# First cross-attention of a two-layer Perceiver step: query keys from 64-row products, a new order for keys and context chunks

## The reference

```python
scale = DH ** (-0.5)                       # DH = 64, HEADS = 16
q = split_heads(x @ Wq)                    # x is layer-normed before
k, v = split(context @ Wkv)                # both split into heads
k = concat(null_key, k); v = concat(null_value, v)
attn = softmax((q * scale) @ k.T)
out = (attn @ v).merge_heads() @ Wout      # then layer norm, residual
```

## Time and profile before

| | us |
|---|---|
| median of 3 runs | 510.11 (509.84 to 511.09) |
| the profiled execution | 510.38 |
| its span | 508.8 |
| TensorE busy (products) | 486.1 |
| VectorE busy | 256.5 |
| ScalarE busy | 233.8 |
| GpSimd busy | 74.4 |

### The profile page before, as it was taken

How to read it: one execution, slowest core, us unless ns; L and a number is a source line. 1 busy time by engine, 2 the same in 40 slices (tenths; PEclk the granted TensorE clock), 3 DMA queues, 4 the chain that set the end, 5 groups by cost and what they waited for, 6 DMA issues and landing times.

```text
span 508.8 us, 8527 instructions
## 1 busy us (share of the span) xinstructions
PE 486.1 (96%) x3600; PEld 415.5 (82%) x3600; DVE 256.5 (50%) x445; ACT 233.8 (46%) x410; POOL 74.4 (15%) x61
## 2 busy tenths in 40 slices
PE   6999999999999999999888999999999999889997
PEld 6987989899988989899775769976666789678697
DVE  2836231337055131310355987866555566358585
ACT  1737332346245233331134967606767353237772
POOL 2112000001010000000110434473000000004342
PEclk9979999999999999999999999999999999999999
DMA  8647000021420000000296999930000074254000
GB/s 320 227 170 250 21 1 1 1 84 50 200 82 1 1 0 1 1 1 2 77 423 265 399 408 408 379 124 1 2 1 1 1 318 180 84 225 189 0 1 10
DMA packets 12325, 62.50 MB, mean 123 GB/s; under 512 B 1183, under 2 KB 3615, under 8 KB 6400
## 3 DMA queue, kind: packets, MB, share of 16 engines
q1 hardware_dynamic: 9696, 52.17, 26.0%
q0 software_dynamic: 2592, 9.80, 5.5%
HBM read 61.84 MB, written 0.13 MB: 122 GB/s over the span
## 4 chain that ended last, share of the span: by engine, by line
PE 79%; DVE 7%; ACT 4%; POOL 4%; issue 3%; DMA 1%; POOLq 1%; SPq 0%; DVEq 0%; ACTq 0%
PE W L1316 18%; PE W L1277 15%; PE W L1460 8%; PE W L1546 6%; PE W L1507 5%; PE W L1214 3%; PE W L1258 3%; PE W L1293 3%; POOL w_lo L489 3%; PE W L1579 3%; PE W L1596 2%; PE W L1338 2%; POOL small L497 1%; ACT w_hi L545 1%; PE W L1351 1%
## 5 line engine op out<-in xcount | busy, mean ns | idle before, releaser
L1316 PE MATMUL W<-probs_turned_hi,ctx_split_hi 128*128 128x256 f32 x256 | 72.8, 285 | 0.1
L1316 PE MATMUL W<-probs_turned_hi,ctx_split_lo 128*128 128x256 f32 x256 | 72.4, 283 | 0.0
L1316 PE MATMUL W<-probs_turned_lo,ctx_split_hi 128*128 128x256 f32 x256 | 72.4, 283 | 0.0
L862 DVE TENSOR_TENSOR probs_turned_lo<-W,probs_turned_hi 128x512 fp32r<-128x512 f32 x32 | 20.6, 687 | 65.0 <-ACT probs_turned_hi L595 65.0
L1277 PE MATMUL W<-ctx_turned_hi,q_keys_hi 128*128 128x512 f32 x128 | 52.4, 409 | 0.0
L1507 PE MATMUL W<-w_hi,acts 128*128 128x256 f32 x272 | 50.8, 286 | 1.5 <-DVE acts L829 1.0
L1277 PE MATMUL W<-ctx_turned_hi,q_keys_lo 128*128 128x512 f32 x128 | 51.0, 398 | 0.0
L1277 PE MATMUL W<-ctx_turned_lo,q_keys_hi 128*128 128x512 f32 x128 | 51.0, 398 | 0.0
L1316 PEld LDWEIGHTS W<-probs_turned_hi,ctx_split_hi 128*128 128x128 f32 x256 | 49.1, 192 | 0.7 <-DVE probs_turned_lo L862 0.5
L1316 PEld LDWEIGHTS W<-probs_turned_lo,ctx_split_hi 128*128 128x128 f32 x256 | 49.1, 192 | 0.2
L1316 PEld LDWEIGHTS W<-probs_turned_hi,ctx_split_lo 128*128 128x128 f32 x256 | 49.1, 192 | 0.0
(11 more groups left out here) (346 smaller groups left out, 909.4 us busy)
## 6 DMA issues: line engine op xcount, KB each, us to landing
arena<-units_dram SPq DMA_DIRECT2D x22, 1024.0 KB, 8.2
ctxmem<-units_dram SPq DMA_DIRECT2D x16, 1024.0 KB, 10.0
fixed<-units_dram SPq DMA_DIRECT2D x7, 1024.0 KB, 7.0
scr<-ctx_dram POOLq DMA_DIRECT2D x4, 512.0 KB, 3.6
pbuf<-ctx_dram POOLq DMA_DIRECT2D x4, 512.0 KB, 5.4
ctxmem<-ctxT_dram SPq DMA_DIRECT2D x2, 1024.0 KB, 14.8
ctxmem<-ctx_dram SPq DMA_DIRECT2D x2, 1024.0 KB, 14.2
scr<-ctxT_dram POOLq DMA_DIRECT2D x3, 512.0 KB, 6.3
```

The costliest lines, as they stand in the source:

```text
L862: dve.tensor_tensor(PT[1][at], bank(4 + c).rearrange("p (t m) -> p t m", t=4), f32(PT[0][at]), ALU.subtract).then_inc(ev("pl_sb"), 1)
L1316: mm = pe.matmul(ps, CXN[a][:, t, c * P:(c + 1) * P], PT[z][:, t, :], start=(t == 0 and n == 0), stop=(t == KEYT - 1 and n == 2))
```

## The change

- q is kept as one tile QF for both batches, without zeros. A key product takes the 64 rows of one head and the 128 tokens of both batches; the two heads of a pair go to two banks. So each pair is computed once, not once per batch: 64 products in all instead of 2 x 32, each over 64 rows.
- Of each pair's result, batch 0 is split into QP at once; batch 1 is copied unsplit (`q_raw`) into the places of used weights and split later, one pair at a turn (LATE_KEYS).
- Only pairs 0 and 1 come ahead of `sim(0)`; 2 and 3 and the null products behind it, 4 and 5 behind `sim(1)`, 6 behind `sim(2)`, 7 behind `sim(3)`.
- SyncE loads x, const, chunk 0, half of `wk0`, chunks 1 to 3, the other half, `wk1`; ScalarE issues `wq`. GpSimd loads chunks from 4 on only.
- Chunk 0 is split ahead of the keys; a score product runs over chunks outside and halves of the keys inside, so that the first needs one chunk at a time.
- Chunks 4 to 9 are split behind the turned probabilities of a row instead of ahead of its exponential; 10 and 11 at the turn. At the turn row 7's probabilities come ahead of the head projection.
- The null products are 32, of 64 rows and 64 columns of q.
- Warm-up: 8 products on a memset tile, then 3 on `const` (before 5 and 9, all on `const`).

```diff
@@ -141,8 +141,13 @@
 CHUNKS, CHUNK = 16, 1024
 TURN = PAIRS
-SPLIT_AT = {0: (4, 5), 1: (6,), 2: (7,), TURN - 1: (8, 9), TURN: (12, 13), TURN + 1: (14,), TURN + 2: (15,)}
-SPLIT_AT_Q = {(b, 2 * k + 1): n for b, first in ((0, 0), (1, 10)) for k, n in enumerate(range(first, 4 + 8 * b))}
+SPLIT_AT = {TURN: (12, 13), TURN + 1: (14,), TURN + 2: (15,)}
+SPLIT_BEHIND = {0: (4, 5), 1: (6, 7), TURN - 1: (8, 9)}
+SPLIT_IN_TURN = (10, 11)
+QK_SET = (2, 1, 3, 2, 2, 3, 3, 2)
+QK_AFTER = {j: 1 + max(i for i in range(j) if QK_SET[i] == QK_SET[j]) for j in range(3, PAIRS)}
+LATE_KEYS = {r: r - 4 if r < TURN else r - 5 for r in range(4, TURN + 5) if r != TURN}
...
+            plan[-1][2].append(("ql_sb", PAIRS + (PAIRS // 2 if unit == "wout" else PAIRS)))
     cycle = list(range(NR, NR + NA + NB))
     units = UNITS[UNITS.index("f1b"):]
...
+            return W[QK_SET[j]][:, :].rearrange("p (h c b q) -> p c h b q", h=2, c=CT, b=B)[:, :, :, b, :]
+        def q_raw(j):
+            at = PLACE["wq" if j < PAIRS // 2 else "wk0"] * UNIT + (j % (PAIRS // 2)) * CT * P
+            return cut(fixed, at, CT, 2, NQ)
+        def q_split(part, j):
+            return QP[part][:, :, j, :].rearrange("p c (h q) -> p c h q", h=2)
         def chunk_of(n, part):
...
+                sync.dma_start(stage_of(n), chunk_src(n)).then_inc(chunk_in(n)[0], 16)
+            def load_keys(half, done):
+                part = slice(half * HALF, (half + 1) * HALF)
+                sync.dma_start(unit("wk0")[:, part], units_in[UNITS.index("wk0")][:, part]).then_inc(ev(done), 16)
+            load_first(0)
+            load_keys(0, "wk0_first")
+            for n in range(1, 4):
+                load_first(n)
+            load_keys(1, f"place{PLACE['wk0']}")
+            load(2)
...
-                    act.wait_ge(ev("qp_ps"), b * PAIRS + j + 1)
-                    act.copy(QP[0][:, :, j, :], qp_bank(j)).then_inc(ev("qh_sb"), 1)
-                    if (b, j) in SPLIT_AT_Q:
-                        keep_hi(SPLIT_AT_Q[b, j])
+            act.dma_start(unit("wq"), units_in[UNITS.index("wq")]).then_inc(ev(f"place{PLACE['wq']}"), 16)
+            keep_xT(bank(4))
+            keep_hi(0)
+            act.wait_ge(ev("qT_ps"), 1)
+            act.mul(QF[:, 0:4], bank(6).rearrange("p (j t) -> p j t", j=4), DH0 ** -0.5).then_inc(ev("qf_sbA"), 1)
+            def keep_q(j):
+                act.wait_ge(ev("qp_ps"), j + 1)
+                act.copy(q_raw(j), q_keys(j, 1)).then_inc(ev("q_raw"), 1)
+                act.copy(q_split(0, j), q_keys(j, 0)).then_inc(ev("qh_sb"), 1)
+            def keep_first_q():
+                act.wait_ge(ev("qp_ps"), 1)
+                act.copy(q_split(0, 0), q_keys(0, 0)).then_inc(ev("qh_sb"), 1)
+                for n in range(1, 4):
+                    keep_hi(n)
+                act.wait_ge(ev("ql_sb"), 1)
+                act.copy(q_raw(0), q_keys(0, 1)).then_inc(ev("q_raw"), 1)
+            def keep_q_hi(j):
+                act.wait_ge(ev("sim_done"), j + 1)
+                act.wait_ge(ev("q_raw"), j + 1)
+                act.copy(q_split(0, j), q_raw(j)).then_inc(ev("qh_sb"), 1)
...
+            keep_first_q()
+            for j in range(1, 4):
+                keep_q(j)
             act.wait_ge(*made("null_sb"))
             for r in range(ROWT + 1):
+                if r == 1:
+                    keep_q(4)
                 if r == TURN:
                     keep_probs_hi(r - 1)
-                    keep_q_hi(1)
+                    for n in SPLIT_IN_TURN:
+                        keep_hi(n)
                     keep_op(r // 2 - 1)
                 if r < ROWT:
                     softmax0(r)
                 if r == TURN:
                     continue
+                if 1 <= r <= 3:
+                    keep_q(4 + r)
                 if r % 2 == 1 and r >= 3 and r != TURN + 1:
                     keep_op((r - 3) // 2)
                 if r >= 1:
                     keep_probs_hi(r - 1)
+                for n in SPLIT_BEHIND.get(r, ()):
+                    keep_hi(n)
+                if r in LATE_KEYS:
+                    keep_q_hi(LATE_KEYS[r])
             keep_op(GROUPS - 1)
...
+            def keep_q_lo(b, j):
+                dve.wait_ge(ev("qh_sb"), b * PAIRS + j + 1)
+                dve.tensor_tensor(q_split(1, j), q_raw(j) if b else q_keys(j, 0), f32(q_split(0, j)), ALU.subtract)\
+                    .then_inc(ev("ql_sb"), 1)
...
+                if r == 0:
+                    for j in (2, 3):
+                        keep_q_lo(0, j)
+                    dve.wait_ge(*made("null_ps"))
+                    dve.tensor_copy(null_s[0:NQ], bank(2)[0:NQ, 0:ROWT])
+                    dve.tensor_copy(null_s[NQ:P], bank(3)[NQ:P, 0:ROWT]).then_inc(*tick("null_sb"))
+                    dve.wait_ge(*made("null_sb"))
                 dve.tensor_scalar(negm[:, r:r + 1], mx[:, r % 2:r % 2 + 1], null_s[:, r:r + 1], -1.0, ALU.max, ALU.mult)\
                     .then_inc(ev("negm_ready"), 1)
                 for n in SPLIT_AT.get(r, ()):
                     keep_lo(n)
+                if r == 1:
+                    keep_q_lo(0, 4)
                 dve.wait_ge(ev("p0_done"), r + 1)
                 z = zs[:, r % 2:r % 2 + 1]
                 step(dve.tensor_tensor(z, stat[:, r, 0:1], stat[:, r, 1:2], ALU.add))
...
-            dve.wait_ge(*made("null_ps"))
-            dve.tensor_copy(null_s, bank(5)[:, 0:ROWT]).then_inc(*tick("null_sb"))
-            dve.wait_ge(*made("null_sb"))
+            keep_q_lo(0, 0)
+            for n in range(1, 4):
+                keep_lo(n)
+            keep_q_lo(0, 1)
             for r in range(ROWT + 1):
                 if r == TURN:
+                    keep_probs_lo(r - 1)
                     keep_heads(r // 2 - 2)
-                    keep_probs_lo(r - 1)
-                    keep_q_lo(1)
+                    for n in SPLIT_IN_TURN:
+                        keep_lo(n)
                 if r < ROWT:
                     softmax0(r)
                 if r == TURN:
                     continue
+                if 1 <= r <= 3:
+                    keep_q_lo(0, 4 + r)
                 if r == 0:
                     dve.wait_ge(ev("const2_in"), 16)
                 if r == 2:
@@ -916,6 +969,10 @@
                     keep_heads(r // 2 - 2)
                 if r >= 1:
                     keep_probs_lo(r - 1)
+                for n in SPLIT_BEHIND.get(r, ()):
+                    keep_lo(n)
+                if r in LATE_KEYS:
+                    keep_q_lo(1, LATE_KEYS[r])
             keep_heads(GROUPS - 1)
             dve.wait_ge(*made("out0_ps"))
...
+            pe.wait_ge(ev("warm_in"), 1)
+            for _ in range(8):
+                pe.matmul(bank(0)[:, 0:P], hn[:, 0:P], hn[:, 0:P], start=True, stop=True)
             pe.wait_ge(ev("const_in"), 16)
-            stay_warm(0, 5)
             turn_x(bank(4), xn)
-            stay_warm(0, 9)
+            stay_warm(0, 3)
...
-                pe.wait_ge(ev("q_sbA"), b + 1)
-                pe.wait_ge(ev("q_sbV"), b + 1)
-                for j in range(PAIRS):
-                    u = "wk0" if j < 4 else "wk1"
-                    wk = unit(u).rearrange("p (j c) -> p j c", j=4)
-                    if b == 0 and j % 4 == 0:
-                        need(u)
-                    if j >= 4:
-                        pe.wait_ge(ev("ql_sb"), b * PAIRS + j - 3)
-                    for c in range(CT):
-                        mm = pe.matmul(qp_bank(j)[:, c, :], wk[:, j % 4, c * P:(c + 1) * P], QB[b][:, j, :],
-                                       start=True, stop=True)
-                    mm.then_inc(ev("qp_ps"), 1)
+                if j % 4 == 3:
+                    mm.then_inc(ev("qT_ps"), 1)
+            def query_keys(j):
+                u = "wk0" if j < 4 else "wk1"
+                wk = unit(u).rearrange("p (j c) -> p j c", j=4)
+                if j == 0:
+                    pe.wait_ge(ev("wk0_first"), 16)
+                    pe.wait_ge(ev("qf_sbA"), 1)
+                if j == 2:
+                    need("wk0")
+                    pe.wait_ge(ev("qf_sbV"), 1)
+                if j == 4:
+                    need("wk1")
+                if j in QK_AFTER:
+                    pe.wait_ge(ev("ql_sb"), QK_AFTER[j])
+                    pe.wait_ge(ev("q_raw"), QK_AFTER[j])
+                for c in range(CT):
+                    for hh in range(2):
+                        rows = slice(hh * DH0, (hh + 1) * DH0)
+                        mm = pe.matmul(W[QK_SET[j]][:, (hh * CT + c) * P:(hh * CT + c + 1) * P],
+                                       wk[rows, j % 4, c * P:(c + 1) * P], QF[rows, j, :], start=True, stop=True)
+                        if j % 4 == 0 and c == hh == 0:
+                            mm.then_inc(ev("units_used"), 1)
+                mm.then_inc(ev("qp_ps"), 1)
...
-                    pe.wait_ge(ev("ql_sb"), (b + 1) * PAIRS)
+                pe.wait_ge(ev("ql_sb"), r + 1)
+                if r == 1:
```

(63 more changed lines are left out.)

64 lines of the change are left out of this document (17 added, 47 removed).

## The result

The changed kernel takes **512.82 us** (median of 20 runs, 509.70 to 513.97) against 509.93 for the kernel before (20 runs, 509.00 to 511.24): ratio 1.0050, 95% interval 1.0037 to 1.0062. It is slower by about half a per cent, where 504.6 was forecast. The profiled execution has a span of 511.2 us, against 508.8.

What follows compares the result with a forecast made beforehand. TensorE, busy 96% of the span, was taken as the bound, on its own work from 52.13 us. Gains of 2.0 (opening) and 3.6 (turn) sum to 5.6 us: 504.6 us, range 500.8 to 509.0.

Steps and rivals of the forecast that it cites:

- The part until the first scores: Opening, steps (a) to (c): first score product ends at 19.8 us instead of 33.5, 13.7 us earlier.
- (b): Opening: wq issued on ScalarE's queue lands at 7.8 us (6.8 to 9); q projection ends at 11.5 instead of 12.8.
- (a): Opening: TensorE warms up on a memset tile from about 1.3 us, ending at 5.3, in time for the turn of x.
- (c): Query keys: 16 instructions of 64 rows, alternating halves, 63 ns apart, 1.0 us a pair; 1.9 without overlap.
- From there to the first attention product: First scores to first attention product: ScalarE and VectorE set the pace; product starts at 50.1 instead of 52.13, 2.0 us left.
- Null products: Opening, null scores: 64 instructions taken at 2.5 us, near L1338; bounds 2.2 and 7.7 us.
- The turn: Transposes to attention product at the batch change: 6.9 us instead of 10.5, 3.6 gained of 7.3 removed.
- The switches between tilings: Some six more mode changes at 0.15 us, 0.9 us, mostly hidden; all exposed, gain about 1.5 us smaller.
- The clock's fall at the turn: Rival, chance 0.33: clock falls at a thin stretch; 508.0 if at the turn, about 507 in the opening.
- The half-height products don't overlap: Rival, chance 0.06: query keys cost 1.9 us a pair, attention product 5 us later; 509.6, no change.
- the dear null products: Null stage at its upper bound, 7.7 us, 5.2 more than taken, plus 3.4 of clock fall: 513; chance 0.06.
- slower: Rival outcome, chance 0.06: the null stage costs its upper bound and brings down the clock; 513 us.

Runs made afterwards that it cites:

- s_wq_sync: Changed kernel with wq issued by SyncE behind const and ahead of chunk 0, instead of by ScalarE at the start: 508.25 us.
- s_wq_waits: Changed kernel with ScalarE issuing wq only after x has landed: 518.63 us.
- t_copy_first: Changed kernel with ScalarE's copies of the attention product's first two parts ahead of the casts of chunks 10 and 11, one each: 510.80 us.
- t_wout_late: Changed kernel with the load of wout waiting for the last late key instead of the fourth: 509.88 us.
- t_split_early: Changed kernel with chunks 8 and 9 split ahead of row 7's exponential again, during the attention product before the turn: 507.35 us.
- o_short_raw: Changed kernel with ScalarE copying only 2 of 64 columns per head of batch 1's unsplit keys, pairs 4 to 7: 511.26 us.

## Why the prediction was wrong

**The part until the first scores: (b) failed.** The text priced when `wq` would land and left out what it would do to x and const, which then shared the engines with it. x landed 5.2 instead of 2.1 us after its issue; `wq` itself, expected at 7.8, landed at 6.6 (5.9 after its issue at 0.74) and was not waited for. (a) gave nothing: the products on the memset tile were through at 4.84, TensorE then idled 3.3 us until the normalised x (8.12), and the projection ran its first part at half pace (4.75 us instead of 3.6). The three products on `const` behind the turn of x, 1.65 us (L1271), now lay on the path too, as `wq` was already there. Together some 4.1 us late at the first keys, and the `s_wq_sync` run gives 3.4 of them back at the attention product. (c) was right: 62 ns apart in the mean, as in the earlier trace rows, 1.0 us a pair (1.12 to 1.16 with the end of the last), first scores 5.88 us.

The half pace does not show in the changed kernel's clock column. Its first part, and below it a stretch of `s_wq_waits` with the same products at a recorded half clock:

```profile
11.00:12.00 1.00, 1.00 (x7) 1.00 (x7) 0.39 (x1) 0.00 (x0) 0.30 (x1) 1.00 1.06 431
```

```profile
15.00:16.00 1.00, 1.00 (x7) 1.00 (x6) 0.00 (x0) 0.00 (x0) 0.00 (x0) 0.50 1.09 434
```

Both have 7 instructions a microsecond, where the kernel before has 11 or 12 in its projection. The trace of the changed kernel has no clock record ahead of 13.24 us, and its instructions go every 213 ns until about then and every 112 behind it: the 1.00 of that stretch is no reading. In the six profiles with the changed kernel's opening the projection took 4.0 to 5.3 us, in the three with `wq` on SyncE and the same products ahead of it 3.8 to 5.0: the same code differs here by over 1 us.

**From there to the first attention product: the sum right, by two misses that cancel.** Null products 1.98 us against 2.5 taken (between 2.2 and 7.7; the narrow-column row was the one to go by, as it said). The 3.4 us by the Trainium skill ("TensorE: Matmul & The Clock Gate", LDWEIGHTS) were too much: the trace shows 31 ns for each of the 64 instructions. They start in pairs, one in each half of the rows, every 58 ns; the 53 ns fit one half, and what the estimate left out is that the halves overlap.
From the end of the first scores to the attention product 30.25 us against 30.3 forecast; the wait ended by row 1's subtraction, as named. The first maximum came 4.4 us behind the scores (forecast 5.5), and from it to the attention product there were 25.9 us (forecast 24.8): that the two differences of 1.1 us cancel is luck. That the opening is not TensorE's alone was right too, and so the late start passed through in full.

**The turn: the start was right, the sum wrong.** 6.7 us until its attention product against 6.9 forecast, ended by the subtraction of row 7. The step that failed is the sentence "Chunks 10 and 11 are loaded only after 8 and 9 are split; they are ready some 12 to 13 us after the turn's start, and the scores want them at 18.4". It let the turn count as 6.9 us and no more, with 3.6 gained. The time was nearly right (cast of chunk 11 at 13.4); the scores are not who waits first. ScalarE's list has the casts of both chunks ahead of the copies that free the attention product's banks, and these are wanted at 12.5. The same text knew that `wout` goes out at "120" and did not set it beside the loads of chunks 10 and 11. Cost: 2.3 us of pause and 1.7 us of half clock, together more than the 3.6 us forecast. `t_copy_first` and `t_wout_late` each remove the pause, `t_split_early` the whole wait.

**The switches between tilings** were priced at 0.9 us, mostly hidden. Nothing larger shows: 1.02 us after the head projection as before, and in the chain keys follow scores (24.03) and null products follow keys (26.02) without a gap.

**The rivals.** The clock's fall at the turn came: in the changed kernel's profile behind the pause of the stall, in `s_wq_sync` and `o_short_raw` behind the thin stretch alone, as the rival had it, and in `t_copy_first` and `t_wout_late` not at all. In other runs it fell in the opening. For the fall in the kernel before, rows 2 and 3 have it at 24.1 us, inside the 32 one-column products (until 25.01) and not behind them. "The half-height products don't overlap" and the dear null products were wrong. The outcome "slower" was given 0.06, for a mechanism that did not occur; the two that did were no rivals at all.

## What to carry to other kernels

A load moved to another queue starts sooner, but everything small and urgent beside it lands later: price the neighbours, not only the load. When a load or a cast is delayed into cover, look for the first reader of anything that stands behind it in the same engine's list, not for the first reader of its data. Work taken from the critical engine pays only if what hid under it is moved out first; here that was one table entry, worth 4 to 5.5 us.

## What the runs showed of the hardware

- Instructions of 64 rows and 128 columns, alternating between the two halves of the rows and two banks, went every 62 ns in the mean (32 in 1.99 us); with a head's four products in one half and then four in the other, every 86 (32 in 2.75 us); at full height, every 118 (64 in 7.55 us). Inside one half they start about 111 ns apart; only neighbours in different halves overlap.
- A load of 1 MB issued at 0.74 us beside x (128 KB) and const (64 KB) from another queue took 5.9 us and stretched theirs from 2.1 and 2.3 to 5.2 and 5.7 us. Issued at 2.96, behind five others, it took 9.3 us itself. A chunk of 0.5 MB issued just ahead of a 1 MB load took 8.2 us, and at most 4.6 without it.
- The clock's falls are not in the same place: at 8 to 9 us, at 24 to 32, at 50, at 122 to 138, once at 400, in none of them in three profiles, each time behind a stretch in which TensorE had idled or run small products. The same stretch need not bring one: behind the null products it fell in five of eleven profiles.
- Executions of one kernel differ by up to 4 us (509.7 to 514.0 for the changed kernel), by 2 in the kernel before. The mean granted clock does not put them in order: the one execution of the changed kernel at 1.000 took 512.2 us, seven at 0.990 took 511.0 to 512.9. A fall can lie where TensorE would have waited anyway, as in `s_wq_sync`, and the slow pace at the start is not in the mean. How much of the spread is the clock's is not shown.
